# A cast of O two steps later, and activation sums ahead of weight lows in two feed-forward bodies

## What is computed

```python
q = layer_norm(x, ln1_g, ln1_b)
qh, kh, vh = (heads(m @ w + b) for m, w, b in ((q, wq, bq), (ctx, wk, bk), (ctx, wv, bv)))
scores = einsum('bqhd,bkhd->bhqk', qh, kh) / sqrt(32)     # masked: a key not after its query
o = einsum('bhqk,bkhd->bqhd', softmax(scores), vh)
x = x + o @ wo + bo
h = layer_norm(x, ln2_g, ln2_b)
out = x + gelu(h @ w1 + b1) @ w2 + b2                       # gelu with erf
```

## Time and profile before

| | us |
|---|---|
| median of 3 runs | 2773.85 |
| lowest and highest | 2772.96, 2775.61 |
| the profiled execution | 2772.35 |
| its span, first to last instruction | 2770.5 |

### The profile page before, as it was taken

How to read it: one execution, slowest core, us unless ns; L and a number is a source line. 1 busy time by engine, 2 the same in 40 slices (tenths; PEclk the granted TensorE clock), 3 DMA queues, 4 the chain that set the end, 5 groups by cost and what they waited for, 6 DMA issues and landing times.

```text
span 2770.5 us, 67361 instructions
## 1 busy us (share of the span) xinstructions
PE 2727.4 (98%) x21928; PEld 2488.9 (90%) x21928; DVE 2041.0 (74%) x5214; ACT 1654.1 (60%) x4017; POOL 890.9 (32%) x842
## 2 busy tenths in 40 slices
PE   8999999999999999999979999999998999999999
PEld 6888888888888888888869999999998999999999
DVE  7777777777777777777698787787788566566556
ACT  5766667666676666766665656656556445444444
POOL 6656566566665666656510000000000000000000
PEclk9999999999999999999999999999999999999999
DMA  5333233332333323333243533534535333343332
GB/s 187 115 131 133 103 125 122 130 131 100 126 122 133 129 99 126 121 133 121 102 161 130 197 153 142 197 141 155 195 126 206 150 151 141 124 167 136 124 156 99
DMA packets 153084, 383.58 MB, mean 138 GB/s; under 512 B 13440, under 2 KB 17536, under 8 KB 144768
## 3 DMA queue, kind: packets, MB, share of 16 engines
q1 hardware_dynamic: 152960, 382.28, 37.2%
HBM read 172.51 MB, written 109.05 MB: 102 GB/s over the span
## 4 chain that ended last, share of the span: by engine, by line
PE 95%; DVE 2%; issue 2%; ACT 1%; POOL 0%; DMA 0%; SPq 0%; DVEq 0%; ACTq 0%; POOLq 0%
PE bank_d L495 19%; PE bank_t L525 11%; PE bank_d L490 7%; PE bank_s L1298 6%; PE bank_s L1299 6%; PE bank_s L1300 6%; PE bank_s L510 6%; PE bank_v L548 5%; PE bank_d L1298 5%; PE bank_d L1300 5%; PE bank_d L1299 5%; PE bank_v L1298 2%; PE bank_v L1300 2%; PE bank_v L1299 2%; PE bank_t L1298 1%
## 5 line engine op out<-in xcount | busy, mean ns | idle before, releaser
L863 ACT ACTIVATE sm<-sm,mins 128x128 f32<-128x128 f32 (+3 forms) x1024 | 572.1, 559 | 439.3 <-DVE mins L670 434.6
L988 POOL TENSOR_SCALAR sm<-sm,recips 128x128 f32<-128x128 f32 (+3 forms) x512 | 549.8, 1084 | 234.5 <-DVE recips L682 232.8
L670 DVE CUSTOM_DVE_ANT_0 sm<-bank_s,mask 128x128 f32<-128x128 f32 (+3 forms) x1024 | 473.5, 483 | 65.5 <-PE bank_s L510 64.2
L615 DVE COPY pT<-bank_t 128x384 f32<-128x384 f32 (+1 forms) x544 | 306.4, 563 | 210.9 <-PE bank_t L525 208.6
L1298 PE MATMUL bank_s<-w_hi,a_hi 128*128 128x256 f32 x1536 | 436.7, 284 | 14.4 <-DVE a_lo L1424 14.4
L1299 PE MATMUL bank_s<-w_lo,a_hi 128*128 128x256 f32 x1536 | 435.8, 284 | 0.0
L1300 PE MATMUL bank_s<-w_hi,a_lo 128*128 128x256 f32 x1536 | 435.7, 284 | 0.0
L525 PE MATMUL bank_t<-ident,sm 128*128 128x128 f32 x2560 | 412.9, 275 | 10.6 <-POOL sm L988 3.4
L525 PEld LDWEIGHTS bank_t<-ident,sm 128*128 128x128 f32 x2560 | 306.6, 140 | 92.3 <-issue 32.7
L1298 PE MATMUL bank_d<-b_hi,w_hi 128*128 128x256 f32 x1280 | 368.9, 288 | 4.5 <-ACT g L1725 2.8
L1300 PE MATMUL bank_d<-b_hi,w_lo 128*128 128x256 f32 x1280 | 363.4, 284 | 0.0
(11 more groups left out here) (161 smaller groups left out, 6542.4 us busy)
## 6 DMA issues: line engine op xcount, KB each, us to landing
stack<-st_hi SPq DMA_DIRECT2D x256, 256.0 KB, 2.4
stack<-st_lo SPq DMA_DIRECT2D x128, 256.0 KB, 2.4
xr<-x_scratch SPq DMA_DIRECT2D x64, 512.0 KB, 4.2
b_scratch<-b_hi SPq DMA_DIRECT2D x16, 1792.0 KB, 9.1
b_scratch<-b_lo SPq DMA_DIRECT2D x16, 1792.0 KB, 12.8
b_hi<-b_scratch SPq DMA_DIRECT2D x16, 1792.0 KB, 7.4
b_lo<-b_scratch SPq DMA_DIRECT2D x16, 1792.0 KB, 11.1
xt<-in_x SPq DMA_DIRECT2D x64, 256.0 KB, 2.6
```

Source lines behind the costliest of these rows:

```text
L615: copy(out, src).then_inc(moved[n % 2], 1)
L670: op = V.tensor_tensor_reduce(sm[:, n % SLOTS_S, off:off + w], bank_s[n % BANKS_S][:, off:off + w], mask[:, 512 - w:512], 1.0, 0.0, ALU.ad ...
L863: op = A.activation(row, row, ACT.Exp, bias=mins[:, g % 2, c:c + 1], scale=-1.0, accum_out=sums[:, g % 2, c:c + 1])
L988: op = G_.tensor_scalar(out=row, in0=row, scalar1=recips[:, g % 2, c:c + 1], scalar2=None, op0=ALU.mult)
```

## The change

Two things. In the attention stage the cast `o_high` of group 3 stands behind the exponential of step 9 instead of 7; other groups as before.

In the feed-forward stage DVE's order in a `first` body changes for d = 1. The low of B21 leaves portion 1 of `w2_parts` and is portion 2; B22 with the sums T2 and T4 is portion 3, and the lows of T2, T3 and T4 are portion 4. Portion 2 stands behind the sum S1 of h = 1 (it stood, with B22, T2 and T4, behind `a_low(0, 1)`), and portions 3 and 4 stand behind `a_low(1, 1)` and the sum S2. In the first body of the second half the four `add_b2` come after them, just ahead of `sum_out` 0; later bodies of the second half have them where they were. ACT's casts of T2 and T4 move behind `a_high(1, 1)` accordingly. No operation is added or removed.

```diff
-    R_AT, PV1_AT, PV0_AT, O_PROD_AT, O_HIGH_AT, O_HIGH_LATE = 4, 5, 9, 6, 7, 11
+    R_AT, PV1_AT, PV0_AT, O_PROD_AT, O_HIGH_AT, O_HIGH_LAST, O_HIGH_LATE = 4, 5, 9, 6, 7, 9, 11
...
-                        if k == (O_HIGH_LATE if g == 1 else O_HIGH_AT):
+                        if k == (O_HIGH_AT, O_HIGH_LATE, O_HIGH_AT, O_HIGH_LAST)[g]:
                             o_high(it, g - 1)
...
             if stage == 1:
                 w_low("T1")
+            if stage == 2:
                 w_low("B21")
-            if stage == 2:
+            if stage == 3:
                 w_low("B22")
                 w_sum("T2")
                 w_sum("T4")
-            if stage == 3:
+            if stage == 4:
                 w_low("T2")
-            if stage == 4:
                 w_low("T3")
                 w_low("T4")
...
             add(c, 1, "C12")
             a_low(c, 0, 1)
+            if switch:
+                w1_parts(4, 0, 1)
+            if ph == 1 and not first:
+                add_b2(c, first, 0)
+            add(c, 1, "C22")
+            if ph == 1 and not first:
+                add_b2(c, first, 1)
+            a_sum(c, "S1", 1)
+            if ph == 1 and not first:
+                add_b2(c, first, 2)
             if first:
                 w2_parts(U + 3, 1, 2)
-            if switch:
-                w1_parts(4, 0, 1)
-            if ph == 1:
-                add_b2(c, first, 0)
-            add(c, 1, "C22")
+            a_low(c, 1, 1)
+            a_sum(c, "S2", 1)
             if first:
                 w2_parts(U + 3, 1, 3)
                 w2_parts(U + 3, 1, 4)
-            if ph == 1:
-                add_b2(c, first, 1)
-            a_sum(c, "S1", 1)
-            if ph == 1:
-                add_b2(c, first, 2)
-            a_low(c, 1, 1)
-            a_sum(c, "S2", 1)
-            if ph == 1:
+                if ph == 1:
+                    for t in range(QT):
+                        add_b2(c, first, t)
+            elif ph == 1:
                 add_b2(c, first, 3)
             sum_out(c, ph, 0)
...
             activate(c, ph, 1, "C12")
-            if first:
-                w2_high(U + 3, 1, ["T2"])
...
             activate(c, ph, 1, "C22")
+            a_high(c, 1, 1)
             if first:
-                w2_high(U + 3, 1, ["T4"])
-            a_high(c, 1, 1)
+                w2_high(U + 3, 1, ["T2", "T4"])
             a_high(c, 2, 0)
```

## The result

The changed kernel takes 2778.43 us, the kernel before 2774.3 us in runs beside it (20 runs each). The ratio is 1.0015 with a 95% interval of 1.0008 to 1.0021: slower by 4.1 us, 2.2 to 5.8 by the interval. That is clear of no change, and small enough (0.15%) to count as the "same" of the forecast. Forecast were +4.95 and 2778.8. Of all executions reported here one, of the kernel with the cast at step 8, took 11433.28 us at a mean granted clock of 0.637, and it is left out of every ratio.

A forecast was written before the change was run, and what follows sets the result against it. PE, busy 98% of the span, bounds the kernel, so only its idle time and low-clock time count. -3.8 + 4.1 + 2.0 + 1.35 + 1.3 = +4.95 on 2773.85 gives 2778.8 us; range 2773.3 to 2783.3.

The forecast's parts named there:

- the "same" of the forecast: Whole-kernel outcome: a time that measurement can't tell from no change, about 0.2% (5.5 us); chance 0.57.
- the terms of order: Effects of the reordered operations themselves: -3.8 us in attention, +4.1 at c = 0, +1.35 at c = 16.
- the rival without a fall of the clock: Feed-forward, c = 0 and c = 16: neither new PE stall is followed by the low clock; +1.65, 2775.5 us; chance 0.12.
- the two terms of the clock: PE at 1.2 GHz behind the new stalls for a_low(2,0): +2.0 us at c = 0, +1.3 us at c = 16.
- Attention: Group 3, first fifteen batches: later cast lets the copy of tile 5 start earlier, 0.25 us per batch; -3.8 us (-3.2 to -4.2).
- The hole of 0.25: Attention, group 3: PE idles 0.25 us before the transposes of tile 7, waiting for ACT's copy of tile 5; it closes.
- The cover: Attention: exp(10) ends 0.2 us later, but tile 10 is transposed over 3 us later, so PE doesn't wait; otherwise 0 gain.
- The rival with the hole left open: Attention, group 3: exp(8) is held by DVE, so the idle gap before tile 7 stays; +8.75, 2782.6 us; chance 0.15.
- Entry: Feed-forward, c = 0: last weight low, SP's load of `xr` and a_low(2,0) come later; PE's third stop ends +4.1 us (3.8 to 4.4).
- Clock behind it, +2.0 forecast: Feed-forward, c = 0: PE's new stall of 5.7 us is followed by 1.2 GHz; +2.0 us (1.3 to 2.6).
- Change of halves: Feed-forward, c = B (c = 16): DVE is the chain and a_low(2,0) comes later; +1.35 us (1.0 to 1.8).
- Clock behind it, +1.3 forecast: Feed-forward, c = B (c = 16): PE's stall of about 2.8 us is followed by the low clock; +1.3 us (0 to 2.3).

The follow-up runs named there:

- entry alone: New order of DVE and ACT at c = 0 only, cast and rest as in the kernel before: 2778.66 us, ratio 1.0019 to the kernel before.
- half load: Changed kernel, but at c = 0 SP loads the first half of `xr` after T3's low and T2's sum: 2775.96 us, ratio 1.0008 to the kernel before.
- halves alone: New order of DVE and ACT at c = 16 only, rest as in the kernel before: 2775.6 us, ratio 1.0009 to the kernel before.
- with the addition: New order at c = 16 only, plus `add_b2(0)` moved behind the add of C22: 2775.32 us, ratio 1.0010 to the kernel before.

## Why the prediction was right

The marks inside the trace bear out the mechanism: the terms of order came as worked out, and both new stops were followed by 1.2 GHz, so the rival without a fall of the clock has fallen. That the time came out 0.4 us from the forecast is in part luck. The change is 4.1 and not 4.95, and the base was 2774.3 in twenty runs where I had 2773.85 from three; and the two terms of the clock were both outside their own ranges in the profile, in opposite directions.

**Attention, -3.8 forecast, -3.4 measured.** The chain on ACT came out as worked out: copy 0.61 behind exp(8), exp(9) 1.08, the cast 1.80 behind it (0.61, 1.08, and about 1.8 forecast). The hole of 0.25 closed, and a batch became 0.23 shorter (86.371 to 86.139 between casts of group 0): I used 0.25 of a range from 0.21 to 0.28. In the last batch nothing was gained, as forecast. The cover held, and no new wait came behind it. The rival with the hole left open has fallen.

**Entry, +4.1 forecast, +4.03 measured.** S1 stands 2.94 behind a_low(0,1) (2.97 forecast), a_low(1,1) 4.37 (4.42), the load 3.68 ahead of `sum_out` 0 (3.69). The stop is 5.98 (5.7). The fit in the Trainium skill, "DMA: Bandwidth & Descriptors", section on the anatomy of one DMA, is made for the GpSimd path and puts a transfer of this size at 3.2, an estimate. This trace shows 3.68 from the issue on SP's queue to the start of `sum_out` 0, half a microsecond more, and the measurement decides.

**Clock behind it, +2.0 forecast (1.3 to 2.6), +1.1 measured, 1.2 with the entry alone.** The fall came as forecast, but the term was mis-sized: I took the price of the two longest stalls, 1.8 and 2.3, and the price doesn't go by the length of the stop. In the windows of the changed kernel the slow stretch is under 4 us, where the one behind the 5.13 stall was 6.2:

```profile
1466.00:1468.00 2.00, 1.81 (x8) 1.84 (x9) 2.00 (x5) 0.00 (x0) 0.00 (x0) 0.50 0.92 326
1468.00:1470.00 2.00, 2.00 (x12) 2.00 (x11) 2.00 (x4) 0.62 (x1) 0.00 (x0) 0.50 0.35 135
1470.00:1472.00 2.00, 2.00 (x18) 2.00 (x18) 1.17 (x3) 0.62 (x1) 0.00 (x0) 0.97 0.03 8
```

Twenty matmuls in 3.8 us (1466.19 to 1470), which at 0.12 would take 2.4: 1.4 lost, of which 1.1 reach c = 16.

**Change of halves, +1.35 forecast, +1.35 measured,** in the whole change and in the part alone. Each operation of DVE stood where the list put it, a_low(2,0) 11.84 behind a_low(0,1).

**Clock behind it, +1.3 forecast (0 to 2.3), +2.5 in the changed kernel, +1.35 in the part alone.** The stop was 4.01 and not 2.8. I had PE arrive 9.0 us after its first release; it came after 7.8, since the low clock that the 5.13 stall leaves behind ended sooner in this execution: about 4.2 us after the release, where it had lasted 6.2. The stop was then followed by a long slow stretch, whose last window before the rise holds 16 matmuls in 3 us:

```profile
2150.20:2153.00 2.80, 2.76 (x13) 2.79 (x14) 2.80 (x5) 0.00 (x0) 0.00 (x0) 0.50 1.02 435
2153.00:2156.00 3.00, 3.00 (x16) 3.00 (x16) 1.56 (x4) 0.88 (x2) 0.00 (x0) 0.50 0.23 96
2156.00:2158.00 2.00, 2.00 (x18) 2.00 (x18) 1.63 (x3) 0.91 (x2) 0.00 (x0) 0.95 0.00 0
```

29 matmuls in 5.8 us, which at 0.12 each would take 3.5: 2.3 lost, near the 2.5 of the ledger. The kernel with half of the residual loaded earlier repeats it: a stop of 4.12 at c = 16, and 625.96 from its release to the end against 623.52, +2.4.

What was wrong in the forecast is thus the size of the two clock terms. The sentence behind them, that every stall of 2.8 us or more is followed by a stretch at 1.2 GHz, held for both new stops but isn't a rule: behind the stall of 2.84 at c = 0 of the changed kernel the granted clock stayed at 1.00. That was worth -0.55 there, a term that the forecast doesn't have, and it hid part of the +2.5.

The three terms of order (-3.8, +4.1, +1.35) are thus right to 0.4 us together. The two terms of the clock, +3.3 forecast, are 3.6 in the whole change's profile and 2.6 as the sum of the parts alone; what they are in the median run is open by about a microsecond.

## What to carry to other kernels

Before an operation is moved past another, list who waits for the last of the group, other queues included: here the weight low wasn't urgent for PE, but a load into its memory waited for it, and its 3.7 us had been covered, all but 1.09 of them, by work that the change moved ahead. Then look where the engine idles and fill that idle time with what is ready; putting "urgent" work first gained little here, since DVE then waited for that work's input, and the small waits of PE that went (0.32 and 0.39) only brought it sooner to the next stop. And judge a step on an in-order engine by what stands directly behind it: two steps later gained 0.23 us a batch, one step later lost 0.28.

## What was not expected of the hardware

The same stop doesn't always bring the clock down, and it doesn't always do so at once. PE's stall of 2.84 us in layer 1 of c = 0 was followed by 1.2 GHz in eight of the nine profiles, and not in the changed kernel. With the cast at step 8 the first matmul behind it took 0.36, the full clock, and the fall came 0.8 us later:

```profile
1438.00:1441.00 3.00, 3.00 (x17) 3.00 (x16) 3.00 (x6) 2.72 (x5) 0.00 (x0) 0.51 1.07 454
```

So a first matmul of 0.36 doesn't show that the stop was free; the windows behind it do. The same holds for the stops of 3.10 and 3.14, which ended at the full clock, with the fall 0.5 and 1.1 us later. In these two bodies all stops of 3.27 us and more ended at the low clock, and none of 2.0 us and less was followed by it. What the stop of 2.84 costs differs too: from it to PE's next wait, for `xn`, it takes 9.89 us where the clock stayed up, 10.45 to 10.61 in five profiles, and 11.46 or 11.47 in three.

What the new stops cost varied from 0.9 to 2.5 us, and not by their length. The last column is how much longer than before the time is from the release to the next mark of the ledger:

| stop for a_low(2,0) | length | low clock behind it, about | cost |
|---|---|---|---|
| entry, changed kernel | 5.98 | 3.9 | 1.1 |
| entry, entry alone | 5.89 | 4.2 | 1.2 |
| entry, half load | 3.27 | 3.4 | 0.9 |
| halves, changed kernel | 4.01 | 6.0 | 2.5 |
| halves, half load | 4.12 | 5.7 | 2.4 |
| halves, halves alone | 3.14 | 3.4 | 1.35 |
| halves, with the addition | 3.10 | 3.4 | 1.4 |

The first stall at c = 16 is 5.13 or 5.14 in all four of the last rows, and the low clock behind it lasted 4.2 and 3.9 us in the two where the stop cost most, 6.2 and 4.9 in the other two. What decides which way it goes, no run here shows.

Executions of one kernel differ in the same manner. In the runs of the halves alone, seven spans lie between 2773.0 and 2773.8 us, with a mean granted clock of 0.996 or 0.997, and four between 2775.7 and 2776.6, with 0.995. The 33 executions of the kernel before that stand beside them spread from 2771.68 to 2775.48 us, with 0.996 to 0.998 in the faster half and down to 0.995 in the slower. So part of the scatter goes with the clock; no trace was taken of the upper four, so the place isn't shown. The profiled execution of the kernel before (0.997) is of the quicker kind and that of the changed kernel (0.995) is not, which fits the 5.8 of the ledger against 4.1 between the medians.

The start of an execution varies by 2.3 us between the nine profiles (first cast of O at 69.5 to 71.8), more than most single terms here. Two profiles are better compared between marks than by their spans.
